# Moving the second product of nine experts out of the expert stage and into the later attention passes

## What is computed

```python
xn = layernorm(x)
q, k, v = xn@Wq.T+bq, xn@Wk.T+bk, xn@Wv.T+bv          # 8 heads, dqk = 2, dv = 16
s = leaky_relu(q.k / sqrt(2), 0.2);  attn = gamma * softmax(s) @ v + xn
# mixture of 16 experts, top 2, capacity 1024 tokens for each expert
t = rmsnorm(xn) * norm_weight
gate, e = top_k(softmax(t @ router.T + router_bias), 2)
slot = position of the token in its expert;  keep = slot < 1024
# expert 0: zero; 1: copy; 2, 3: constant vectors; 4..15: an MLP
h = gelu(rows @ fc1[e].T + b1[e])                      # 128 -> 512
o = h @ fc2[e].T + b2[e]                               # 512 -> 128
ffn = sum over the kept choices of gate * o / sum of kept gates
out = x + attn + ffn
```

## Time and profile before

| what | value |
|---|---|
| median of three runs | 944.16 us (942.27 to 945.29) |
| span of the profiled execution | 940.0 us |
| TensorE busy | 861.2 us, 92% |
| VectorE busy | 735.3 us, 78% |
| ScalarE busy | 691.3 us, 74% |
| GpSimd busy | 601.5 us, 64% |
| moved by DMA | 59.36 MB, mean 63 GB/s |

### The profile page before, as it was taken

The page is one execution under the profiler, slowest core; times in us unless marked ns, Lnnn a source line. Parts: engine busy times, 40 slices in busy tenths (PEclk is TensorE's granted clock), DMA queues, the critical chain, the costliest instruction groups (busy, mean ns, idle before and its releaser), DMA issues. The chain is left out here.

```text
span 940.0 us, 20061 instructions
## 1 busy us (share of the span) xinstructions
PE 861.2 (92%) x7499; PEld 348.9 (37%) x7500; DVE 735.3 (78%) x859; ACT 691.3 (74%) x811; POOL 601.5 (64%) x610
## 2 busy tenths in 40 slices
PE   0688269999999999999999999999999999999997
PEld 0444112222222224776867732222222222222222
DVE  5788889999999994101011099999999999999996
ACT  0578888888888887444453568888888888888886
POOL 3355247777777663999999226657567575765782
PEclk9999659999999999999999999999999999999999
DMA  7833101111111112233242210102112111210202
GB/s 214 303 66 74 32 27 33 51 40 51 47 27 36 25 38 88 90 121 116 93 138 71 94 44 22 40 19 59 36 25 59 25 36 29 70 29 13 69 18 55
DMA packets 71225, 59.36 MB, mean 63 GB/s; under 512 B 33770, under 2 KB 58178, under 8 KB 71136
## 3 DMA queue, kind: packets, MB, share of 16 engines
q1 hardware_dynamic: 61520, 48.06, 17.6%
q0 software_dynamic: 8192, 9.37, 3.6%
q10 hardware_dynamic: 1424, 0.76, 0.3%
HBM read 31.58 MB, written 30.02 MB: 66 GB/s over the span
## 5 line engine op out<-in xcount | busy, mean ns | idle before, releaser
L1133 DVE TENSOR_SCALAR ps<-ps 128x1024 f32<-128x1024 f32 x512 | 600.1, 1224 | 14.6 <-PE ps L825 11.7
L718 ACT ACTIVATE pr<-ps 128x1024 f32<-128x1024 f32 x512 | 523.4, 1023 | 104.5 <-PE ps L835 72.9
L855 PE MATMUL ps<-pr,vp 128*32 128x256 f32 x4096 | 327.2, 392 | 0.1
L835 PE MATMUL ps<-q,kz 64*128 64x512 bf16 x1024 | 200.7, 389 | 10.2 <-DVE ps L1133 4.4
L825 PE MATMUL ps<-q,kz 62*128 62x512 bf16 x1024 | 200.3, 389 | 2.9 <-DMA q<-parts_dram 1.3
L505 POOL DMA_INDIRECT xs<-eout,idxs x128 | 129.0, 1008 | 105.0 <-ACT pr L718 75.5
L490 POOL DMA_INDIRECT disp<-xn,idx x128 | 125.9, 984 | 50.8 <-issue 29.2
L835 PEld LDWEIGHTS ps<-q,kz 64*128 64x128 bf16 x1024 | 49.0, 93 | 225.7 <-DVE ps L1133 188.4
L1152 DVE TENSOR_TENSOR pr<-ps,parts 128x1024 f32<-128x1024 f32 x12 | 14.7, 1225 | 149.6 <-PE ps L920 149.6
L855 PEld LDWEIGHTS ps<-pr,vp 128*32 128x32 f32 x4096 | 81.1, 108 | 119.4 <-issue 117.6
L744 ACT ACTIVATE pr<-ps,b1s 128x512 f32<-128x512 f32 x96 | 65.8, 687 | 53.7 <-PE ps L909 53.7
(11 more groups left out here) (122 smaller groups left out, 530.3 us busy)
## 6 DMA issues: line engine op xcount, KB each, us to landing
moved<-att SPq DMA_DIRECT2D x480, 8.0 KB
disp<-pr SPq DMA_DIRECT2D x12, 512.0 KB, 4.9
eout<-pr SPq DMA_DIRECT2D x12, 512.0 KB, 2.9
y<-in_x SPq DMA_DIRECT2D x8, 512.0 KB, 8.1
out<-y SPq DMA_DIRECT2D x7, 512.0 KB
w<-in_w1t SPq DMA_DIRECT2D x12, 256.0 KB, 3.2
w<-in_w2t SPq DMA_DIRECT2D x12, 256.0 KB, 3.4
xs<-disp SPq DMA_DIRECT2D x6, 512.0 KB, 4.9
```

The costliest lines, as they stand in the source:

```text
L718: act.activation(pr[:, c % BUFS, 2 * pair:2 * pair + 2, :], ring[i % RING], ACT.Exp, scale=SLOPE).then_inc(S["exps"], 1)
L835: last = pe.matmul(ring[i % RING][:, k, :], kz[r:r + TILE, hg, pair, kc * P:(kc + 1) * P], q2[r:r + TILE, hg, qh * HALF:(qh + 1) * HALF], ...
L855: last = pe.matmul(acc[p % 2][32 * g:32 * g + 32, cols], vp[:, hg, kc, g, :], pr[:, c % BUFS, g % PAIRS * 2 + g // PAIRS, cols], start=(kc ...
L1133: dve.tensor_scalar(s, s, 0.0, 1.0 / SLOPE - 1.0, ALU.max, ALU.mult).then_inc(S["relu"], 1)
```

## The change

- Experts 3, 7 and 11 (`WHOLE`) are computed in the expert stage as before. For the nine others (`LATER`) the gelu's output is stored to DRAM (`hsd`, 1 MB for each half of an expert, from three buffers `hs`). In each of the passes 12 to 29 (`later_at`) TensorE makes the second product of one half: 16 products in the 12 units from `TURN` on (`second`, called in `attention` behind `values`), into the accumulator that the pass does not use. SyncE loads the half a pass ahead (`load_half`), with the second weights and bias once per expert. ScalarE copies the sums to `raw` behind the first exponential of the next pass (`half_out`), GpSimd adds the bias, multiplies by the gate and sends four adding indirect DMAs (`add_half`).
- Output rows are added by adding DMAs to `moe` in DRAM, one row for a token, which is zeroed in pass 1. For this a scattered row carries its gate and its token number, in two more columns (`xr`, `CR` = 130), and slots without a token have a spare row. The scatter goes over all first choices, then over all second ones.
- The 128 gathers and their weighting are gone. Instead, in passes 30 and 31, SyncE loads `moe` in eight pieces (`fetch_sums`, two buffers), GpSimd adds them to `y` (`sums`), and all sequences are stored there (before: as they became complete, `STORES`).
- The copies with a scale (`take_turned`) go from ScalarE to VectorE, the transposes are issued in two halves between the first products (`turn_half`), and half of the plain experts' work goes from GpSimd to VectorE (`KEPT` = 4 of 8 groups). Loops over experts are unrolled.

SyncE's part, which orders the transfers:

```diff
+            load_expert(1)
+            for e in range(E_MLP):
+                if e in LATER:
+                    for half in range(2):
+                        g = 2 * e + half
+                        sp.wait_ge(S["gel"], 2 * FC * e + FC * (half + 1))
+                        sp.dma_start(hsd[2 * LATER.index(e) + half, :, :], hs[g % 3].rearrange("p f m -> p (f m)")
+                                     ).then_inc(S[f"hst{g % 3}"], 16)
+                if e + 2 < E_MLP:
+                    sp.wait_ge(S["gel"], 2 * FC * (e + 1))
+                    sp.wait_ge(S["etr"], 2 * (e + 1))
+                    sp.wait_ge(S["gid"], 2 * (e + 1))
+                    load_expert(e + 2)
...
             for p in range(BH * NPB, B * NPB):
                 operands_in(p)
+                if later_at(p - 1) is not None and later_at(p + 1) is not None:
+                    load_half(later_at(p + 1))
+                if p == B * NPB - 1:
+                    for n in range(2):
+                        fetch_sums(n)
+                    for n in range(3):
+                        store_sequence(n)
+                        fetch_sums(n + 2)
                 if p > BH * NPB:
                     spread(p - 1)
-                if p % NPB == 0 and p > BH * NPB:
-                    for s in STORES[p // NPB - BH - 1]:
-                        store_sequence(s)
-            for s in STORES[B - BH - 1]:
-                store_sequence(s)
+            for n in range(3, B):
+                store_sequence(n)
+                if n + 2 < B:
+                    fetch_sums(n + 2)
```

TensorE's part:

```diff
                     if i > first + PAIRS:
                         values((i - 3) // PAIRS, (i - 3) % PAIRS)
+                    p, r = divmod(i - TURN, UP)
+                    if r < SPAN2 and later_at(p) is not None:
+                        for k in range(UP):
+                            if k * SPAN2 // UP == r:
+                                second(later_at(p), k)
...
+            def second(q, k):
+
+                d, half = divmod(q, 2)
+                j, f = divmod(k, FC)
+                if k == 0:
+                    pe.wait_ge(S["turned"], BH * NPB + q)
+                    pe.wait_ge(S[f"lh{q % 2}"], 16 * (3 * (d + 1) if half == 0 else d + 1))
+                    pe.wait_ge(S["lh0"], 16 * 3 * (d + 1))
+                mm = pe.matmul(acc[(q + 1) % 2][:, j * P:(j + 1) * P],
+                               hq[q % 2][:, f * HALF + j * P:f * HALF + (j + 1) * P],
+                               w2q[d % 2][:, f * C:(f + 1) * C], start=(f == 0), stop=(f == FC - 1))
+                if k == UP - 1:
+                    mm.then_inc(S["f2"], 1)
```

GpSimd's part in the later attention:

```diff
+            def sums(s):
+
+                pool.wait_ge(S[f"mb{s % 2}"], 16 * (s // 2 + 1))
+                wait_done(pool, "y_att", added)
+                pool.sem_inc(S["carry"], 1)
+                yt = y[:, bass.ts(s, TB), :]
+                pool.tensor_tensor(yt, yt, mb[s % 2].rearrange("p (t c) -> p t c", c=C), ALU.add).then_inc(S["comb"], 1)
+
+            def gather(p, results):
+
+                q = later_at(p - 1)
+                if q is not None:
+                    add_half(q)
+                if p > BH * NPB + 1:
+                    pool.wait_ge(S["exps"], UP * p + LATE)
                     pool.sem_inc(S["carry"], 1)
...
+                results()
+                if p == B * NPB - 2:
+                    for s in range(3):
+                        sums(s)
+                if p == B * NPB - 1:
+                    for s in range(3, B):
+                        sums(s)
```

More of the change, by code:

```diff
@@ L59 @@
 BUFS = 4
-GB = 2
 TURN = 5
+SPAN2 = 12
+KEPT = 4
 BLOCK = 32
@@ L346, in _ @@
                 operands_in(p)
+                if p == 1:
+                    for n in range((T + SPARE) // M):
+                        sp.dma_start(moe[bass.ts(n, M), :].rearrange("(p j) c -> p (j c)", p=P),
+                                     ddr[:, 0, :, :].rearrange("p j c -> p (j c)")[:, 0:M]).then_inc(S["moe_zero"], 16)
                 if 0 < p < BH * NPB - 1:
@@ L528, in gather, with add_rows @@
[L528 to L545 removed]
+            def add_rows(e, j, rows, done):
+                pool.indirect_dma_start(
+                    out=moe, out_offset=bass.IndirectOffsetOnAxis(ap=token_of[:, e, j:j + 1], axis=0),
+                    in_=rows, in_offset=None, compute_op=ALU.add).then_inc(S[done], 16)
@@ L756, in _ @@
             ready(ACT.Gelu)
-            with act.Fori(0, E_MLP // 2 - 1) as k:
-                for u in range(2):
-                    expert(2 * k + u, u, False)
-            for u in range(2):
-                expert(E_MLP - 2 + u, u, u == 1)
+            for e in range(E_MLP):
+                expert(e)
             ready(ACT.Exp)
@@ L901, in expert @@
-            def expert(e, u, first=False, last=False):
-                pe.wait_ge(S["edt"], 2 * (e + 1))
+            def second(q, k):
+                d, half = divmod(q, 2)
+                j, f = divmod(k, FC)
[8 more added lines that the diff above has]
+                    mm.then_inc(S["f2"], 1)
@@ new lines, in turn_half, with turn_rows, expert @@
+            def turn_half(e, half):
+                pe.wait_ge(S[f"ed{e % 2}"], 16 * loads_of(e))
+                wait_done(pe, "edt", 2 * (e - 1) + half + 1)
+                for t in range(4):
+                    last = pe.transpose(ps[:, half, t * P:(t + 1) * P], ddr[:, e % 2, half * 4 + t, 0:C], ident)
+                last.then_inc(S["etr"], 1)
+            def turn_rows(e):
+                for half in range(2):
+                    turn_half(e, half)
+            def expert(e):
+                u = e % 2
@@ L927, in _ @@
             ahead(0, AHEAD)
             attention(0, BH)
-            for u in range(2):
-                expert(u, u, first=u == 0)
-            with pe.Fori(1, E_MLP // 2 - 1) as k:
-                for u in range(2):
-                    expert(2 * k + u, u)
-            for u in range(2):
-                expert(E_MLP - 2 + u, u, last=u == 1)
+            for e in range(E_MLP):
+                expert(e)
             attention(BH, B)
```

387 lines of the change are left out of this document (237 added, 150 removed).

## The result

The changed kernel takes 1047.07 us (median of four runs, 1044.92 to 1051.10) against 943.72 (four runs); the ratio is 1.111, with a 95% interval from 1.108 to 1.115. It is 103 us slower. The prediction was 1019 with a range up to 1045: the direction was right, the size was 28 us short, and the time lies 2 us outside the range.

A forecast was written before the change was run, and what follows sets the result against it. TensorE alone bounds the expert stage; TensorE and VectorE are both nearly full in the later attention. From 940.0 us, -30 + 1 + 79 + 25 = +75 gives 1015, or 1019 as run median; range 975 to 1045.

The forecast's parts named there:

- Step (c): Passes 12 to 29: inserted second products make TensorE the bound, pass 23.8 against 19.4 us, +79 us.
- my upper bound: Passes 12 to 29: each place shows 0.1 us more and a little waiting, 5.6 us a pass, 101 us.
- C: Passes: inserted products fit into TensorE's waits, pass stays 19.4 us, total 940 us; chance 0.11.
- D: Late adding transfers or parked loads hold TensorE 1 to 3 us at each pass's first insertion: 1040 to 1070; chance 0.07.
- A: Expert stage: transfers overlap, loads landing beside the store, stage gains 55 to 64 us, total 985 to 994; chance 0.12.
- B: End: shorter because fetches start earlier than SyncE's order seems to let them, total 992 to 1000; chance 0.08.
- Step (a): Expert stage: nine second products gone, then the store-and-load chain limits; gain 30 us, bounds 64 and 15.
- Step (d): End: sums come back late through a serial chain of fetches and additions, +25 us, bounds 17 and 33.
- Step (b): Before the experts: zero fills, wider rows and reordered scatters stay hidden, cost 0; without that cover 5 us.

The follow-up runs named there:

- the repaired kernel: Changed kernel with one block of products a pass, expert loads moved ahead, eight fetches starting pass 31, later reciprocal: 986.9 us, 1.048 of the kernel before.

## Why the prediction was right in kind and short in size

**The sum of it.** The 64.3 us of second products taken from the stage come back as 18 x 3.53 = 63.5 us in the passes, if we take the price of one place. TensorE had nothing to give on either side, so this trade is zero. The 103 us are what came on top: 43.2 us of the stage's gain that did not show (64.3 - 21.1), 30.4 at the end, 19.6 for twelve places instead of one (18 x 1.09), 5.4 for ScalarE's copy and the other company (18 x 0.30), 1.8 where the attention begins anew, 3.4 before the experts; less the 0.8 that the trade leaves.

**Step (c), mis-sized: 89 us instead of 79.** That TensorE becomes the bound, the order of the units and the gap of 0.57 us behind the values were right. The price of a place was not. I took 0.20 + (2n - 1) x 0.1116 us from the middle of a train of 32 instructions; in each of the 216 places the second instruction starts 0.21 us behind the first, and a place costs 0.20 + 0.22 n. That is 0.11 us too little for each of twelve places, 1.3 us a pass. The rest of such a unit then took 1.11 us instead of 1.14, and the four other units 1.28 instead of 1.38, which gave 0.75 back. What my upper bound adds, one more instruction time a place, is what happened. The rule of the Trainium skill ("TensorEngine Tiling (Array Packing)", "Key Properties") that a change of tiling mode drains the engine agrees with what the runs with fewer places showed, 1.09 us a pass between twelve places and one; how much of the 0.20 us of a place is a drain, no run separates.

**The rivals fell.** C: the products did not fit into TensorE's waits; three quarters and more of a place show, even at the turn. D: TensorE stood idle before none of the 216 places. A: the stage gained 21 us, not 55 to 64. B: the end is 30 us longer.

**Step (a), mis-sized: -21 us instead of -30.** The waits are where the chain from the last gelu through the store to the loads has them, and reordering it gave 12 and 23 us back. Between the last first products of experts 0 and 11 I had 132.7 us, and the trace has 141.9. The 9.2 us more split as follows.

- *The clock, put at nothing: some 11 us.* I had looked at the stall alone, not at what the engine does after it. From the transposes behind a stall to the last first product I counted 2.24 us; undisturbed it is 2.21, but behind six of the eight stalls it was 3.0 to 4.3 (4.3 at 440.12, where the granted clock was 0.50 from 440 to 442 us), 9.5 us in all, and twice the gelu ended 0.8 to 0.9 us late, behind a last product of 1.6 to 1.7 us instead of 0.86. All first products together took 97 us instead of 84.7. Keeping TensorE busy gave 4 to 6 us of this back.
- *The adding transfers of whole experts, put at nothing: some 4 us.* I wrote of them "Nothing of that is on the path". GpSimd sends those of experts 3 and 7 from 426 to 442 and from 480 to 495 us, beside the loads of the rows of experts 6 and 10; the periods in which TensorE waits for these rows are 15.2 and 15.0 us long, where I had 11.2. These rows took 7.3 us from issue to landing, where the six others behind a store took 4.8 to 5.0; all eight kernels in which SyncE's order in the stage is unchanged show 7.0 to 7.9 for these two and at most 6.3 for the others. No run leaves the adding transfers out, so that they are the cause is likely, not shown.
- *Loads that took less than I gave them* brought back 1.5 us in each of the three periods with a broadcast bias and 0.4 in three others. That my 13.2 us for these periods (13.3, 12.5 and 13.4 measured) came out is luck: a shorter wait and slow products cancelled.

Issues from 432 to 441 us, KB and us to landing, kernel after:

```profile
ddr<-disp SPq DMA_DIRECT2D x1, 520.0 KB, 7.3
moe<-pr,token_of POOLq DMA_INDIRECT x6, 6.8
```

VectorE, to which I gave its operations at 1.2 us, had them at up to 3.3, waiting for GpSimd's, and was late with two takes (0.86 us at 382 us); in this kernel that is small, with the loads repaired it is part of the next bound.

**Step (d), mis-sized: +30 us instead of +25.** Fetches landed after 5.4 us in the median, not 3.7, and they began 1.7 us later in pass 31 than I had counted. The order in which things waited was as written.

**Step (b), cost at nothing: +3.4 us.** I wrote that GpSimd waits for unit 7 of pass 0, and did not ask who waits for GpSimd. VectorE does: the reciprocal that moved into its stream of rectifying stands in front of unit 7 and waits for the last of GpSimd's routing operations. Timeline of VectorE, kernel after:

```profile
140.48 0.55 DVE L1281 RECIPROCAL gsum<-gsum 128x64 f32<-128x64 f32 x1 [2.02 <-POOLq L705]
```

From the first scores to the first turn this costs 1.5 us (31.6 against 30.1), and the repaired kernel, in which the reciprocal stands four units later, wins it back. The other 2.0 us had come up before the attention began; their cause stays open, and they may be the spread from run to run: the first scores stand at 124.6 to 127.3 us in the kernels of this document, and at 123.8 in the one before.

**The range.** Four terms were short on the same side, by 3 to 10 us each. Each stayed within its own bounds (15 for the stage, 101 for the passes, 33 for the end, 5 before the experts), and these bounds together reach 1069; but my range ended at 1045, room for one term at its bound and not for four that err the same way. I think that they did because each was counted with the engines at their pace in the undisturbed kernel.

## What to carry to other kernels

Before work is moved from a stage that an engine bounds, read that same engine's slack in the stage that receives it, in its own starts: two nearly full stages of one engine have nothing to trade, and the transport, the switches and the collection at the end are then pure cost. A stall can have a second price behind it, here most likely the lower clock, and a queue that is relieved of one wait shows the next thing queued on it. If small foreign work must be put into a finely woven loop, put it in as one block.

## What the runs showed of the hardware that was not expected

- A float32 product of 128 x 128 x 128 costs 0.22 us in a block of 1, 2, 4 or 16 (0.42, 0.64, 1.09 and 3.77 us), plus 0.20 us for the block, between values on column tiles and scores on row tiles.
- An additive indirect transfer holds GpSimd for 1.57 us, a plain scatter for 0.98 (128 rows of 512 bytes against 520).
- VectorE and GpSimd operations on [128, 1024] float32 in SBUF wait for each other: of VectorE's 32 in the expert stage, the 14 that began during one of GpSimd's ended 1.08 to 1.09 us behind it (2.1 to 3.3 us in all, alone 1.2); GpSimd's additions took 2.17 us alone and 2.9 to 3.1 when they began during one of VectorE's. VectorE's copies out of PSUM took 0.75 us in either case.
- Eight 512 KB fetches issued one after the other hold SyncE's queue for 12.5 us (290 to 331 GB/s in that time), and whatever stands behind them waits; spread over the end of the kernel after, a fetch is issued in 0.49 us in the median.
